# A padded copy of the edge attributes, and the last edge pass with its weights also in PSUM, weighed column by column between the carried sums

## The reference, cut to what matters

```python
e = (edge_attr @ We).reshape(-1, H, C)
k_j = k[src] + e
v_j = v[src] + e
alpha = jnp.sum(q[dst] * k_j, axis=-1) / jnp.sqrt(jnp.float32(C))
amax = jax.ops.segment_max(alpha, dst, num_segments=n)
ex = jnp.exp(alpha - amax[dst])
denom = jax.ops.segment_sum(ex, dst, num_segments=n)
out = jax.ops.segment_sum(v_j * (ex / denom[dst])[:, :, None], dst, num_segments=n)
```

## Time and profile before

| | us |
|---|---|
| median of 3 runs | 5683.37 (5675.45 to 5690.65) |
| span of the profiled execution | 5673.3 |
| first graph passes, about | 325 to 2451 |
| last edge pass, about | 3504 to 5150 |

### The profile page before, as it was taken

The page is one execution under the profiler, slowest core; times in us unless marked ns, Lnnn a source line. Parts: engine busy times, 40 slices in busy tenths (PEclk is TensorE's granted clock), DMA queues, the critical chain, the costliest instruction groups (busy, mean ns, idle before and its releaser), DMA issues. The chain is left out here.

```text
span 5673.3 us, 49658 instructions
## 1 busy us (share of the span) xinstructions
PE 2860.0 (50%) x13052; PEld 2232.1 (39%) x13052; DVE 3824.3 (67%) x6117; ACT 1441.9 (25%) x2526; POOL 3388.4 (60%) x3382
## 2 busy tenths in 40 slices
PE   7513200000000000015899986888888888884777
PEld 5412200000000000014677633777776777673456
DVE  7357778786454545546543464989899998995763
ACT  1113333332233333311222211222222222221320
POOL 0267777777777777753440276777777777773200
PEclk9655555555555555556799998999999999896888
DMA  3133344432363333323232355999999999993114
GB/s 101 36 84 108 107 130 148 130 104 83 103 220 110 109 110 109 110 87 124 93 124 68 107 191 191 317 319 323 319 319 321 319 323 318 323 318 113 67 47 148
DMA packets 290231, 961.79 MB, mean 170 GB/s; under 512 B 79248, under 2 KB 119831, under 8 KB 248468
## 3 DMA queue, kind: packets, MB, share of 16 engines
q0 software_dynamic: 171296, 483.60, 28.6%
q1 hardware_dynamic: 118788, 476.59, 24.9%
HBM read 626.03 MB, written 345.69 MB: 171 GB/s over the span
## 5 line engine op out<-in xcount | busy, mean ns | idle before, releaser
L1249 PE MATMUL e_psE<-e_we,e_eaT 128*128 128x256 f32 x3136 | 903.5, 415 | 279.3 <-DVE e_wv L1148 179.3
L1111 POOL DMA_INDIRECT e_kv<-kv,rec x784 | 875.7, 1117 | 266.3 <-issue 253.7
L779 POOL DMA_INDIRECT g_g<-t,rec x784 | 777.1, 991 | 254.0 <-issue 253.7
L779 POOL DMA_INDIRECT g_g<-t,dst_of x784 | 743.6, 949 | 259.3 <-issue 257.2
L1249 PEld LDWEIGHTS e_psE<-e_we,e_eaT 128*128 128x128 f32 x3136 | 649.4, 210 | 400.7 <-ACT e_eaT L1192 299.4
L1407 PE MATMUL j_psM<-ident,tail 128*128 128x128 f32 x32 | 7.2, 416 | 1149.0 <-PEq L53 1149.0
L1250 PE MATMUL e_psE<-e_kv,ident 128*128 128x256 f32 x1568 | 509.8, 409 | 0.0
L816 DVE TENSOR_TENSOR_SCAN g_wv<-g_fx,g_wv 128x2176 f32<-128x2176 f32 x98 | 459.0, 4684 | 0.2 <-issue 0.2
L1407 PEld LDWEIGHTS j_psM<-ident,tail 128*128 128x128 f32 x32 | 6.8, 322 | 1149.8 <-issue 1149.8
L1118 POOL DMA_INDIRECT e_q<-q,q_of x392 | 370.9, 946 | 119.7 <-issue 119.7
L956 ACT ACTIVATE g_st<-g_wv 128x2048 f32<-128x2048 f32 x98 | 375.9, 3836 | 0.0
(11 more groups left out here) (519 smaller groups left out, 6620.8 us busy)
## 6 DMA issues: line engine op xcount, KB each, us to landing
state<-e_st SPq DMA_DIRECT2D x98, 1088.0 KB, 6.2
e_ea<-in_edge_attr SPq DMA_DIRECT2D x98, 896.0 KB, 9.8
state_f<-g_st SPq DMA_DIRECT2D x49, 1088.0 KB, 4.4
state_b<-g_st SPq DMA_DIRECT2D x49, 1088.0 KB, 4.3
m_work<-xs SPq DMA_DIRECT2D x119, 128.0 KB, 2.3
ys<-m_work SPq DMA_DIRECT2D x119, 128.0 KB, 1.7
xs<-g_ta SPq DMA_DIRECT2D x28, 512.0 KB
g_g<-t,rec POOLq DMA_INDIRECT x784
```

What stands on the lines that cost most here:

```text
L779: pool.indirect_dma_start(g[:, u, j, :], None, tab, bass.IndirectOffsetOnAxis(ap=at_, axis=0)).then_inc(gat[u], 16)
L1111: pool.indirect_dma_start(kv[:, u, b, :], None, c.kv, bass.IndirectOffsetOnAxis(ap=c.rec[:, t, 1:2], axis=0)).then_inc(gkv[u][b // 4], 16)
L1249: nc.tensor.matmul(half, eaT[:, m, j, k, :], we[:, k, :], start=(k == 0), stop=False)
```

## The change

Four things change.

1. **The copy.** `ea_tail` becomes `ea_p`, a copy of the attributes of all 128 partitions, with room for 785 instead of 784 rows in each. The first graph passes make it: one or two partitions with each of the 98 blocks, 128 in all, in place of one partition with each of 16 blocks. The edge pass loads a block's attributes from `ea_p` in a single DMA of 128 partitions, and the choice between two sources is gone.
2. **The weights.** ScalarE takes the exponentials twice, first into a PSUM bank `cwp`, then into `cw` as before. The bank comes from `psT`, which has three instead of four; the fourth turn waits until ScalarE has copied the first.
3. **The order on VectorE.** The multiplication of 2048 columns becomes eight of 256 with `cwp`, and these stand between the sums. In place of the drains the sums wait on a semaphore, `scaled`, that each raises when it is complete.
4. **The carried maximum.** ScalarE copies it behind the exponentials; VectorE waits for it ahead of the sum by head.

```diff
-                ea, lo = A["edge_attr_256"], (112 + a) * T
+            def copy_attributes(p):
+                ea, lo = A["edge_attr_256"], p * T
+                real = min(T, E - lo)
+                spread = lambda at, n: c.ea_p[p:p + 1, at * D:(at + n) * D].rearrange("o (a n) -> (o a) n", a=16)
...
-                if 0 <= blk - FIRST < 16:
-                    others += copy_attributes(blk - FIRST)
+                for p in range(blk * P // NB, (blk + 1) * P // NB):
+                    others += copy_attributes(p)
...
-        psT = [pb(f"psT{n}") for n in range(4)]
+        psT = [pb(f"psT{n}") for n in range(3)]
+        cwp = pb("cwp")[:, 0:H * B1].rearrange("p (h b) -> p h b", h=H)
...
-                with sp.If(unsorted > 0):
...
-                    sp.dma_start(ea[0:112, u, :, :], rows(A["edge_attr_256"][0:112 * T, :])).then_inc(eg[u], 16)
-                    sp.dma_start(ea[112:P, u, :, :], rows(c.ea_tail)).then_inc(eg[u], 16)
+                sp.dma_start(ea[:, u, :, :], c.ea_p[:, bass.ds(b * (B * D), B * D)]).then_inc(eg[u], 16)
...
-                    v.wait_ge(marked, blk + 1)
-                    copy(at[:, :, 0], mt[:, :, B])
-                    v.drain()
...
+                        if half:
+                            v.wait_ge(scaled, blk * B1 + 1)
...
+                    v.wait_ge(marked, blk + 1)
+                    v.wait_ge(carried, blk + 1)
...
+                    of_head = lambda b: cwp[:, :, b].unsqueeze(2).to_broadcast([P, H, C])
+                    last_row = lambda b: st[:, u, b - 1, 0:D] if b else before[:]
+                    def weigh(b):
+                        return tt(by_head(wv[:, b, :]), by_head(wv[:, b, :]), of_head(b + 1), ALU.mult)
+                    def add_to_row(b):
+                        v.wait_ge(scaled, blk * B1 + b + 2)
+                        return nc.vector.scalar_tensor_tensor(out=st[:, u, b, 0:D], in0=last_row(b), scalar=kept[:, u, b:b + 1],
+                                                              in1=wv[:, b, :], op0=ALU.mult, op1=ALU.add)
...
+                    v.wait_ge(cwpd, blk + 1)
+                    weigh(0)
+                    tt(by_head(before[:]), by_head(st[:, 1 - u, B - 1, 0:D]), of_head(0), ALU.mult).then_inc(scaled, 1)
+                    weigh(1)
                     v.wait_ge(cwd, blk + 1)
...
+                    tt(cw[:, :, 0], cw[:, :, 0], den[:, :, B], ALU.mult).then_inc(opened, 1)
                     v.wait_ge(free, blk + 1)
                     for b in range(B):
...
-                        if b < B - 1:
-                            v.drain()
-                    last.then_inc(std, 1)
+                        add_to_row(b).then_inc(scaled, 1)
+                        if b + 2 < B:
+                            weigh(b + 2)
+                        if b == 0:
+                            v.wait_ge(opened, blk + 1)
+                            nc.vector.tensor_tensor_scan(flat(den[:]), flat(kept_h[:, u]), flat(cw[:]), 0.0, ALU.mult,
+                                                         ALU.add).then_inc(dnd, 1)
...
+                nc.scalar.activation(cwp.rearrange("p h b -> p (h b)"), ex[:].rearrange("p h b -> p (h b)"),
+                                     ACT.Exp).then_inc(cwpd, 1)
...
+                nc.scalar.activation(at[:, :, 0], mt[:, :, B], ACT.Copy).then_inc(carried, 1)
...
+                        if m == 3:
+                            pe.wait_ge(tcp, blk * 4 + 1)
...
-    c.ea_sorted = dram("ea_sorted", (EP, D))
-    c.ea_tail = dram("ea_tail", (16 * T, D))
+    c.ea_p = dram("ea_p", (P, (T + 1) * D))
```

More of the change, by code:

```diff
@@ L704, in _ @@
             others = 0
[L706 removed]
+            def copy_attributes(p):
+                ea, lo = A["edge_attr_256"], p * T
+                real = min(T, E - lo)
+                spread = lambda at, n: c.ea_p[p:p + 1, at * D:(at + n) * D].rearrange("o (a n) -> (o a) n", a=16)
                 over_engines = lambda rows: rows.rearrange("(a n) w -> a (n w)", a=16)
[L708 to L710 removed]
+                sp.dma_start(spread(0, real), over_engines(ea[lo:lo + real, :])).then_inc(other, 16)
                 if real == T:
                     return 1
[L713 removed]
+                sp.dma_start(spread(real, T - real), over_engines(ea[0:T - real, :])).then_inc(other, 16)
                 return 2
@@ L1048, in edge_pass @@
         st = sb("st", [P, U, B, SW])
-        ld, gq0, gq1, eg0, eg1, used, exd, cwd, dnd, std, so0, so1, free, dump, tp, tcp, ep, ed = (
-            sem(n) for n in ("ld", "gq0", "gq1", "eg0", "eg1", "used", "exd", "cwd", "dnd", "std", "so0",
+        ld, gq0, gq1, eg0, eg1, used, exd, cwd, dnd, so0, so1, free, dump, tp, tcp, ep, ed = (
+            sem(n) for n in ("ld", "gq0", "gq1", "eg0", "eg1", "used", "exd", "cwd", "dnd", "so0",
                              "so1", "free", "dump", "tp", "tcp", "ep", "ed"))
@@ L1055, in edge_pass @@
         marked, act_mt = sem("marked"), sem("act_mt")
+        cwpd, carried, scaled, opened = (sem(n) for n in ("cwpd", "carried", "scaled", "opened"))
         block = s.enter_context(nc.Block())
@@ L1065, in _ @@
             sp.sem_inc(free, 1)
-            unsorted = c.flag_on(sp)
             def load_attributes(b, u):
-                at_ = bass.ds(b * (B * D), B * D)
-                rows = lambda a: a.rearrange("(p t) w -> p (t w)", t=T)[:, at_]
-                with sp.If(unsorted > 0):
-                    sp.dma_start(ea[0:112, u, :, :], rows(c.ea_sorted[0:112 * T, :])).then_inc(eg[u], 16)
-                    sp.dma_start(ea[112:P, u, :, :], rows(c.ea_sorted[112 * T:EP, :])).then_inc(eg[u], 16)
-                with sp.Else():
-                    sp.dma_start(ea[0:112, u, :, :], rows(A["edge_attr_256"][0:112 * T, :])).then_inc(eg[u], 16)
-                    sp.dma_start(ea[112:P, u, :, :], rows(c.ea_tail)).then_inc(eg[u], 16)
+                sp.dma_start(ea[:, u, :, :], c.ea_p[:, bass.ds(b * (B * D), B * D)]).then_inc(eg[u], 16)
             def store(i, u):
                 blk = i * U + u
-                sp.wait_ge(std, blk + 1)
+                sp.wait_ge(scaled, (blk + 1) * B1 + 1)
                 sp.wait_ge(act_mt, blk + 1)
@@ L1129, in _ @@
                 nc.vector.memset(kept_h[:, u, :, 0], 0.0)
-            nc.vector.memset(at[:], -BIG)
-            nc.vector.memset(mt[:], -BIG)
+            nc.vector.memset(at[:], -BIG).then_inc(carried, 1)
             v.drain()
@@ L1134, in _ @@
             v.sem_inc(ed, 4)
+            v.sem_inc(scaled, 1)
             with v.Fori(0, NBLK // U) as i:
@@ L1213, in one_block @@
                                      ACT.Copy).then_inc(act_mt, 1)
-                act.wait_ge(std, blk + 1)
+                act.wait_ge(scaled, (blk + 1) * B1 + 1)
                 if later:
@@ L1238, in turn @@
                                 o = (2 * j + k) * P
-                                last = nc.tensor.transpose(psT[m][:, o:o + P], ea[:, u, 2 * m + j, k * P:(k + 1) * P],
+                                last = nc.tensor.transpose(psT[m % 3][:, o:o + P], ea[:, u, 2 * m + j, k * P:(k + 1) * P],
                                                            c.ident[:])
```

19 lines of the change are left out of this document (3 added, 16 removed).

## The result

The changed kernel takes 5558.66 us (5557.4 to 5560.09, four runs), the kernel before beside it 5682.01 (5675.45 to 5690.65, four runs): a ratio of 0.9788, 95% interval 0.9776 to 0.98. Forecast were 5564 us and a range of 5531 to 5630.

A forecast was written before the change was run, and what follows sets the result against it. VectorE was taken as the bound, GpSimd next, DMA third. From 16.57 to 15.3 us per block, 1.27 times 97 blocks is 123 us, less 4 for copies, 119 off 5683.4: 5564 us, range 5531 to 5630.

The forecast's parts named there:

- VectorE sets the pace, GpSimd is just behind: Last edge pass before the change: VectorE sets the period of 16.57 us per block, GpSimd next limit, DMA third.
- VectorE 15.13 us: VectorE's time per block after the change: 8.50 us plus a new tail of 6.63 where 8.07 stood.
- the head: VectorE's part of a block from L1147 to the start of the weighing at L1166, taken as 8.50 us.
- five pairs: VectorE's tail: five turns of sum and weighing at 0.34 + 0.34 us each, 3.40 us per block.
- The wait ahead of the reduction: VectorE's new waits ahead of L1151, costed at nothing because the work of L1147 and L1148 covers them.
- the rival that it shows through: VectorE's pairs: semaphore wait with register arithmetic shows, a pair takes 0.80 us, VectorE 15.85, time 5617; chance 0.14.
- the one that pairs do not overlap: VectorE's pairs: each operation starts only when the last is complete, 0.91 us a pair, 27 us slower, 5710; chance 0.06.
- GpSimd 15.2 us: GpSimd per block: 12 gathers, 15.0 us, plus 0.2 of smaller stalls, as the PSUM operand removes the long ones.
- DMA falls from 16.57 to 13.7 because of the pad: Edge pass: padded pitch makes attribute reads as fast as gathers, so DMA needs 13.7 us per block, not 16.57.
- the pad changes nothing: Attribute reads stay slow for another reason, DMA stays at 16.57 us per block, time 5687; chance 0.08.
- The copies, +4 us: First gather pass: 112 more row copies, mostly hidden, two rows bare at the end, 4.2 us; bounds 0 to 12.
- The 0.1 us for two nearly equal loops that catch each other: Allowance per block above GpSimd's 15.2 us for VectorE and GpSimd delaying each other, giving 15.3.

The follow-up runs named there:

- pad_alone: Kernel before the change with only the padded copy of all partitions and the single attribute load, VectorE code untouched: 5688.87 us, ratio 1.0023.
- sbuf_weights: Changed kernel, but the weighings read `cw` in SBUF instead of `cwp` in PSUM: 5618.79 us, ratio 0.9897.
- weights_ahead: Changed kernel, but all eight weighings stand ahead of the first sum and the sums follow each other: 5624.23 us, ratio 0.9914.
- no_pad: Changed kernel, but the attribute copy has no room for a 785th row, pitch 784 KB as before: 5558.92 us, ratio 0.9799.
- old_loads: Changed kernel, but attributes copied and loaded as before: 16 partitions copied, two DMAs of 112 and 16 per block: 5580.98 us, ratio 0.9825.

## Why the prediction was right, point by point

**VectorE sets the pace, GpSimd is just behind.** Right as to DMA, by pad_alone: lighter DMA alone moved nothing. Between the two engines pad_alone does not decide, as its gathers (eight of 1.141 and four of 0.946 us, each with 0.305 ahead) fill the 16.57 too; in the kernel before they fill 16.40 (1.119 and 0.946). That GpSimd was so near was due to gathers stalled beside VectorE's work, so the two were coupled already, and the change had to relieve both (sbuf_weights and weights_ahead each relieve one).

**VectorE 15.13 us.** Measured 15.25, in terms: the head 8.59 for 8.50 (4213.67 to 4222.26); three operations 1.00 for 1.02; first sum, weighing and scan 0.94 for 0.90; five pairs 3.62 for 3.40; from the last two sums to the next head 1.02 on average (1.12 and 0.92) for 1.23; the opening of the denominator 0.08 in both. Two sizes were off. The wait ahead of the reduction, counted at nothing because the halves would cover it, shows: the reduction starts 1.49 us after the last half (4217.07 to 4218.56), in pad_alone, which hasn't got it, 1.35 (4209.50 to 4210.85). And a pair is 0.73 us, not 0.68: the weighing is the 0.33 that was taken, the sum is 0.40 and not 0.34, because its price was carried over from another operation. The semaphore itself costs nothing there; the rival that it shows through (0.80) and the one that pairs do not overlap (0.91) are out. That operations overlap is seen directly: a weighing starts 0.40 us after a sum that lasts 0.48.

**GpSimd 15.2 us.** Right: 24 gathers of 1.25 and 0.47 of longer ones are 30.47 for two blocks, and sbuf_weights shows that the PSUM operand is why.

**DMA falls from 16.57 to 13.7 because of the pad.** Wrong in three ways. The pad is not the cause (no_pad); one DMA of 128 partitions is. The 16.57 was no floor: with the old loads 15.42 was reached, so a load of ten tenths did not show that DMA could do no more. And the load fell to 95.5%, not below 9.5 tenths, at 349 GB/s where some 345 were forecast. The time of the rival "the pad changes nothing", 5687, falls with it: its condition holds, its price does not. The slow loads that the prediction read out of the 245 GB/s of the earlier trace rows were there, but not because of the pitch. The figures of the Trainium skill, "DMA: Bandwidth & Descriptors", section "Latency and other measured facts", that the prediction set against it are of copies between tensors in HBM, the main memory, and the 214 GB/s belong to a padded pitch of 4 MiB; they pointed the right way all the same, as no_pad shows no loss at 784 KB. That the forecast came out in spite of this was luck: the single DMA came along with the pad, and slow loads were worth only some 20 us.

**The copies, +4 us.** It was 11 us by pad_alone and 10.4 in the profile; the bounds 0 to 12 hold it. The end cost 4.5 us (9.88 for 5.41) against 4.2, as forecast. The rest can't be told from what lies between profiles. From the first gather of the first passes to their last it is 2096.7 us before and 2102.0 in the changed kernel, but also 2104.7 in old_loads, which has the copies of before. The 0.04 us per block was read from blocks with one copy; where two meet the last gathers VectorE is idle for 6.8 us in place of 6.0, and the blocks with one copy, with 5.7, make up for part of it.

**Sum.** Taken were 15.3 per block and 4 us, -119; in the profile it was 15.24 per block, -129.8, and +12.9 ahead of the pass, -116.9. The 0.1 us for two nearly equal loops that catch each other was not needed, though the two are tied as nearly as forecast. That and the first passes nearly cancel, which is luck as well.

## What to carry to other kernels

Two loops on two engines that meet in every block are one bound: removing work from either alone showed nothing here, so change both, and then test by taking a piece from each and from both. When dependent operations wait for each other, put independent ones between them; when an operand slows a neighbour engine, look where it lies. Load SBUF with all 128 partitions in a single DMA, as 112 and 16 or 64 and 64 were slower here; do not copy a count of rows such as 127, which ran on one engine; and do not take a DMA load of ten tenths for a floor until a lighter load has moved the time.

## What the runs showed of the hardware that was not expected

An 8 KB packet into SBUF lasts 309 ns in a DMA of 128 partitions, 496 in 112 and 16, and 566 in two of 64, from the same tensor. A copy of 127 rows ran on one engine at 27 GB/s, and the store behind it in SP's queue held SP for 43 us. The slow packets brought the load to 102% and cost 0.2 us of 15.2 per block. And kernels with the same first passes differ there by up to 17 us between their profiles, 0.3% of the whole time.
